# A two-stage attention and FFN kernel: the first tile's attention brought forward by one slot

## What is computed

```python
local_out  = softmax(q1 @ k1.T * scale) @ v1                          # full attention, one head of 128
sparse_out = softmax(top_k(q2 @ k2.T * scale, 102)) @ v2              # only the 102 largest scores of a row
mem_out    = [xp, softmax(xp @ bank.T) @ bank] @ mem_out_w + b        # 64 memory rows
pred_out   = gelu((h @ pred1_w + b)) @ pred2_w + b
s = concat(local_out, sparse_out, mem_out, pred_out) @ warboss_w + warboss_b
g = silu(relu(xn @ w1 + b1) @ w2 + b2)                                # FFN, width 2048
out = x + s * g
```

## Time and profile before

| what | value |
|---|---|
| median of 3 runs | 2587.35 us |
| profiled execution | 2589.47 us |
| its span (first to last instruction) | 2587.7 us |
| mean granted TensorE clock | 0.993 of full speed |
| chain that ended last | PE 94%, DVE 4%, DMA 1%, POOL 1% of the span |
| PE busy | 2535.0 us, 98% |
| DVE busy | 2317.5 us, 90% |
| ACT, POOL busy | 1363.0 us (53%), 1118.1 us (43%) |
| DMA | 558.60 MB, mean 216 GB/s |

### The profile page before, as it was taken

How to read it: one execution, slowest core, us unless ns; L and a number is a source line. 1 busy time by engine, 2 the same in 40 slices (tenths; PEclk the granted TensorE clock), 3 DMA queues, 4 the chain that set the end, 5 groups by cost and what they waited for, 6 DMA issues and landing times.

```text
span 2587.7 us, 37027 instructions
## 1 busy us (share of the span) xinstructions
PE 2535.0 (98%) x12900; PEld 2149.0 (83%) x12900; DVE 2317.5 (90%) x5194; ACT 1363.0 (53%) x2311; POOL 1118.1 (43%) x862
## 2 busy tenths in 40 slices
PE   6999999889999999999999999999999999999998
PEld 5888888778888888888888888888888888888886
DVE  7666666589999999999999999999999999999996
ACT  5777777634444444444444444444445454444443
POOL 4445554423444444444444444444444444444444
PEclk9999999989999999999999999999999999999999
DMA  6887788774566456645664566456645654565454
GB/s 217 302 306 296 294 311 305 294 267 155 196 213 217 163 196 214 214 166 196 216 215 164 196 215 214 165 197 215 214 164 196 213 210 163 196 230 200 165 201 166
DMA packets 166776, 558.60 MB, mean 216 GB/s; under 512 B 18048, under 2 KB 31040, under 8 KB 158144
## 3 DMA queue, kind: packets, MB, share of 16 engines
q1 hardware_dynamic: 166592, 556.24, 60.9%
HBM read 421.96 MB, written 134.22 MB: 215 GB/s over the span
## 4 chain that ended last, share of the span: by engine, by line
PE 94%; DVE 4%; DMA 1%; POOL 1%; ACT 0%; issue 0%; POOLq 0%; SPq 0%; ACTq 0%
PE acc L59 9%; PE acc L61 9%; PE acc L60 9%; PE hid L61 9%; PE hid L59 9%; PE hid L60 9%; PE ps L59 5%; PE ps L61 5%; PE ps L60 5%; PE o L59 5%; PE o L61 5%; PE o L60 5%; PE scores L1299 4%; PE scores L59 2%; PE scores L61 2%; PE scores L60 2%
## 5 line engine op out<-in xcount | busy, mean ns | idle before, releaser
L1052 POOL TENSOR_TENSOR h_lo<-h,h_hi 128x512 fp32r<-128x512 f32 x256 | 333.7, 1304 | 866.6 <-ACT h_hi L950 865.4
L1192 DVE MAX8 top_l<-larger 128x8 f32<-128x512 f32 x832 | 576.4, 693 | 13.2
L1212 DVE MATCH_REPLACE8 larger<-top_l,larger 128x512 f32<-128x512 f32 x768 | 521.6, 679 | 0.0
L949 ACT ACTIVATE h<-hid,small 128x512 f32<-128x512 f32 x256 | 176.5, 690 | 483.3 <-PE hid L61 483.3
L59 PE MATMUL acc<-w2s,h_hi 128*128 128x512 f32 x1024 | 412.1, 402 | 0.0
L59 PE MATMUL hid<-xnT,w 128*128 128x512 f32 x1024 | 400.3, 391 | 4.4 <-DMA w<-ffn_scratch 4.4
L61 PE MATMUL hid<-xnT,w 128*128 128x512 f32 x1024 | 400.5, 391 | 0.0
L61 PE MATMUL acc<-w2s,h_lo 128*128 128x512 f32 x1024 | 400.3, 391 | 0.0
L60 PE MATMUL acc<-w2s,h_hi 128*128 128x512 f32 x1024 | 400.2, 391 | 0.0
L60 PE MATMUL hid<-xnT,w 128*128 128x512 f32 x1024 | 400.0, 391 | 0.0
L1052 POOL TENSOR_TENSOR pT_s<-pT,pT_s 128x512 fp32r<-128x512 f32 x256 | 326.7, 1299 | 52.5 <-ACT pT_s L962 52.5
(11 more groups left out here) (175 smaller groups left out, 5593.5 us busy)
## 6 DMA issues: line engine op xcount, KB each, us to landing
w2s<-ffn_scratch SPq DMA_DIRECT2D x259, 512.0 KB, 3.9
w<-ffn_scratch SPq DMA_DIRECT2D x258, 512.0 KB, 4.2
tl<-tile_scratch SPq DMA_DIRECT2D x66, 512.0 KB, 3.9
xnT_scratch<-xnT SPq DMA_DIRECT2D x16, 2048.0 KB, 13.6
kv_scratch<-kv_out SPq DMA_DIRECT2D x32, 1024.0 KB, 5.6
tile_scratch<-tiles_out SPq DMA_DIRECT2D x16, 2048.0 KB, 8.3
xnT<-xnT_scratch SPq DMA_DIRECT2D x64, 512.0 KB, 7.0
xin<-in_L_attn_x SPq DMA_DIRECT2D x17, 1024.0 KB, 9.1
```

The costliest lines, as they stand in the source:

```text
L949: nc.scalar.activation(h32[:, c % 2, :], hid[:, :], ACT.Relu, bias=bias)
L1052: return nc.gpsimd.tensor_tensor(out_, value, hi_.bitcast(F32), ALU.subtract).then_inc(ready, 1)
L1192: l_step = count(nc.vector.max(top_l[:, own], larger[:, :]))
L1212: l_step = count(nc.vector.match_replace(larger[:, :], top_l[:, own], larger[:, :], LOWEST))
```

## The change

The attention of a tile runs one slot ahead of its FFN.

- The first tile's sparse scores are computed on PE after job `qs` of half 14, its local scores after job `pi` of half 15. DVE does its search in pieces between the jobs of these two halves (`first_search`, a generator, one round for each `next`): 1 round after gelu's low part of half 14, 3 after its `xnT` low parts, then 1, 1, 1, 2 and 4 rounds at five places of half 15. ACT copies the scores, and does both exponents and the scaling of the local ones.
- For this the `scores` banks, the search's tensors and the first inputs live through both stages (`Shared`). Stage 1 has 6 PSUM banks for its jobs instead of 8. `xin` and `xn` of stage 1 lie in the tensor `early`, which in stage 2 holds scores and probabilities. `xnT32` is gone; the transposed rows are written straight to where their low part goes (`xnT_raw`).
- The last half has no `tr` jobs; SP loads half 0's transposed rows back from scratch instead (`first_slot`), with `tl1` and `w1_0`. `tl0`, `ks` and `kl` are loaded in halves 13 and 14. The layer norms of halves 16 and 17, and their input loads, are gone. The last value part is made by POOL as the others are.
- Stage 2 runs slots 1 to 63 with the FFN chunks of F = m - 1, and a slot 64 that has only FFN chunks (4 f1, 5 f2) beside the last tile's transposes, products and mixes. `sums_of_half` moves with the FFN from slots with T modulo 4 = 0 to slots with T modulo 4 = 1. Gates and residuals are five slots behind instead of four. `mixed` has three buffers instead of two. Residuals of the last two tiles are done by DVE with their own input loads.

```diff
-BANKS = 8
+BANKS = 6
...
+    ORDER = [(n, name) for n in range(HALVES) for name in JOBS if n < LAST or name[:2] != "tr"]
+    PLACE = {job: KT + i for i, job in enumerate(ORDER)}
...
# stage 1, SP
-                        if n == LAST:
-                            load_first()
+                        if n == LAST:
+                            first_slot()
...
+                        if n == LAST - 2:
+                            first_tile()
+                        if n == LAST - 1:
+                            first_local()
...
# stage 1, ACT, after a job was read
+                            if (n, name) == (LAST - 1, "qs"):
+                                act.wait_ge(shared.ss_done, 1)
+                                nc.scalar.activation(shared.sc(), scores[:, :], ACT.Copy, scale=SCALE)\
+                                    .then_inc(shared.sc_ready, 1)
+                            if (n, name) == (LAST, "ms"):
+                                act.wait_ge(shared.nml_ready, 1)
+                                nc.scalar.activation(shared.prob(0), scores[:, :], ACT.Exp, bias=nml[:, :], scale=SCALE,
+                                                     accum_out=sums[:, 0:1]).then_inc(shared.el_ready, 1)
+                                act.wait_ge(shared.nms_ready, 1)
+                                nc.scalar.activation(shared.prob(1), shared.sc(), ACT.Exp, bias=nms[:, 0:1])\
+                                    .then_inc(shared.es_ready, 1)
+                            if (n, name) == (LAST, "qs"):
+                                act.wait_ge(shared.invl_ready, 1)
+                                nc.scalar.activation(shared.prob(0), shared.prob(0), ACT.Copy, scale=inv[:, 0:1])\
+                                    .then_inc(shared.pl_ready, 1)
...
# stage 1, DVE
+                        if n == LAST:
+                            dve.wait_ge(shared.sl_done, 1)
+                            nc.vector.tensor_reduce(mxl[:, :], scores[:, :], AX_X, ALU.max).then_inc(shared.nml_step, 1)
...
+                            next(rounds)
...
                         nc.vector.tensor_reduce(nmx[:, :], mscore[:, :, :], AX_X, ALU.max,
                                                 negate=True).then_inc(max_ready, 1)
+                        if n == LAST:
+                            next(rounds)
...
+                        if n == LAST:
+                            dve.wait_ge(shared.el_ready, 1)
+                            nc.vector.reciprocal(inv[:, 0:1], sums[:, 0:1]).then_inc(shared.invl_ready, 1)
+                            next(rounds)
                         dve.wait_ge(bank_read, done(n, "p1b"))
...
+                        if n == LAST:
+                            next(rounds)
+                            next(rounds)
                         dve.wait_ge(bank_read, done(n, "wt"))
...
# stage 1, PE, after a job
+                            if (n, name) == (LAST - 1, "qs"):
...
+                                first_scores(T_QS, shared.ks, shared.ss_done)
+                            if (n, name) == (LAST, "pi"):
...
+                                first_scores(T_QL, shared.kl, shared.sl_done)
...
# stage 2, SP, before the slots
                 load_w1(1, 1)
-                sp.wait_ge(tiles_st, 16 * 2 * B)
+                sp.wait_ge(tiles_st, 16 * HALVES)
                 load_w2(0, 0)
-                load_kv(U_KL, 0)
                 load_w2(1, 1)
-                load_tl(1, 1, 1)
-                sp.wait_ge(kv_st, 16 * 4 * B)
+                load_tl(2, 2, 2)
+                sp.wait_ge(kv_st, 32 * HALVES)
+                load_w2(2, 2)
+                load_kv(U_VL, 0)
...
# stage 2, DVE, search
-                        if r == R_SUMS and T % HTILES == 0 and not known_first(m, 1):
-                            sums_of_half(2 * b + T // HTILES - 1)
-                        if r == R_GATE and not known_first(m, HTILES):
-                            gates(m - HTILES, T % HTILES)
+                        if r == R_SUMS and T % HTILES == 1 and not known_first(m, 5):
+                            sums_of_half((m - 5) // HTILES)
+                        if r == R_GATE and not known_first(m, 5):
+                            gates(m - 5, (m - 5) % HTILES)
...
# stage 2, DVE, after slot 63
+                apply_threshold(SLOTS - 1, TILES - 1)
+                gates(SLOTS - 1 - HTILES, HTILES - 1)
+                mix(SLOTS - 2)
+                mix(SLOTS - 1)
+                sums_of_half(HALVES - 1)
                 for t in range(HTILES):
-                    gates((B - 1) * TILES + HTILES + t, t)
-                mix(B * TILES - 2, HTILES - 2)
-                mix(B * TILES - 1, HTILES - 1)
+                    gates(SLOTS - HTILES + t, t)
+                for m in range(SLOTS - 2, SLOTS):
+                    t = m % HTILES
+                    dve.wait_ge(gate_ready, m + 1)
+                    nc.vector.tensor_tensor(gate[:, t, :], gate[:, t, :], mixed_of(m), ALU.mult).then_inc(last_prod, 1)
...
+                    nc.vector.tensor_tensor(gate[:, t, :], gate[:, t, :], residual_of(m), ALU.add).then_inc(fin_last, 1)
...
# stage 2, PE, slot 64
+                f1(C, c, h)
                 pe.wait_ge(ps_ready, m - 1)
                 transposes(1)
-                f2(B * BC - 1, BC - 1, 2 * B - 1)
+                f2(C - 1, c - 1, h)
+                f1(C + 1, c + 1, h)
 
                 pe.wait_ge(pT_h, 4 * g + 2)
                 pe.wait_ge(ps_ready, m)
                 transposes(2)
+                f2(C, c, h)
+                f1(C + 2, c + 2, h)
                 pe.wait_ge(mix_ready, m - 2)
                 head_out(g, U_VS)
+                f2(C + 1, c + 1, h)
+                f1(C + 3, c + 3, h)
                 pe.wait_ge(at_l, g + 1)
                 mix(m - 2, (m - 2) % TL_RING)
+                f2(C + 2, c + 2, h)
                 pe.wait_ge(mix_ready, m - 1)
                 mix(m - 1, (m - 1) % TL_RING)
+                f2(C + 3, c + 3, h)
```

More of the change, by code:

```diff
@@ L538, in steps @@
+                rounds = first_search()
                 def steps(b):
@@ L607, in bank_projection, with first_scores @@
                     pe.wait_ge(sm_split, 2)
-                    product(nc, ps[:, BANKS - 1, 0:P], bkT_s[:, 0, :, :], bkT_s[:, 1, :, :], sm_hi[:, 1, :],
+                    product(nc, scores[:, 0:P], bkT_s[:, 0, :, :], bkT_s[:, 1, :, :], sm_hi[:, 1, :],
                             sm_lo[:, 1, :], True, True).then_inc(bm_ps, 1)
                 bank_projection()
+                def first_scores(slot, keys, ready):
+                    tl0 = shared.tl0
+                    for j in range(2):
+                        last = product(nc, scores[:, j * 512:(j + 1) * 512], tl0[:, HI, slot, :], tl0[:, LOW, slot, :],
+                                       keys[:, j, HI, :], keys[:, j, LOW, :], True, True)
+                    last.then_inc(ready, 1)
                 def steps(b):
@@ L928, in _ @@
+                for m in range(1, SLOTS + 1):
+                    slot(m)
+                for m in (SLOTS - 2, SLOTS - 1):
+                    load_x(m)
+                for m in range(SLOTS - HTILES, SLOTS):
+                    store(m)
                 for t in range(HTILES):
@@ L1037, in _, with slot @@
-                for b in range(B):
-                    slots(b)
-                last = B * TILES - 1
+                def slot(m):
+                    T, F = m % TILES, m - 1
+                    C = c = HC * F
+                    sparse_scores(m, T % 2)
+                    chunk(C, c)
+                    sparse_probabilities(m - 1, 1 + (T - 1) % 2)
+                    transposed(m - 1, 0)
+                    chunk(C + 1, c + 1)
+                    if T % 2 == 0:
+                        transposed(m - 1, 1)
+                        sparse_exponents(m, T)
+                        if not known_first(m, 5):
+                            gates(m - 5, (m - 5) % HTILES)
+                        chunk(C + 2, c + 2)
+                        local_exponents(m)
+                        head_out(m - 1, 1)
+                        local_probabilities(m)
+                    else:
+                        sparse_exponents(m, T)
+                        if not known_first(m, 5):
+                            gates(m - 5, (m - 5) % HTILES)
+                        local_exponents(m)
+                        local_probabilities(m)
+                        chunk(C + 2, c + 2)
+                        transposed(m - 1, 1)
+                    chunk(C + 3, c + 3)
+                    if T % 2 == 1:
+                        head_out(m - 1, 0)
@@ L1040, in _ @@
+                for m in range(1, SLOTS):
+                    slot(m)
+                last = SLOTS - 1
+                C = c = HC * last
+                chunk(C, c)
                 sparse_probabilities(last, 1 + last % 2)
                 transposed(last, 0)
+                chunk(C + 1, c + 1)
                 transposed(last, 1)
-                for t in range(2):
```

(31 more changed lines are left out.)

680 lines of the change are left out of this document (356 added, 324 removed).

## The result

| | before | after |
|---|---|---|
| median of the runs, us | 2587.35 | 2598.54 |
| lowest and highest | 2586.85 to 2587.92 | 2597.91 to 2600.36 |
| profiled execution: its time, span | 2589.47, 2587.7 | 2600.15, 2598.3 |
| slots 5, 9, ... 61, us each | 32.00 to 32.08 | 33.43 to 33.45 |
| the other slots from 2 on | 31.88 to 31.93 | 31.88 to 31.93 |

The change makes the kernel slower: the ratio is 1.0045, with a 95% interval of 1.0033 to 1.0057. The forecast was 2593.4 us, with a range of 2580 to 2601. So the direction holds, and the size is +11.2 us where +6.0 was forecast.

What follows compares the result with a forecast made beforehand. PE was taken to set the time in mid stage 2, with DVE 2.4% behind. Terms +19.1 (sums), 0 (banks), -31.6 (boundary) and +18.5 (tail) gave +6.0 on 2587.35, so 2593.4 us, range 2580 to 2601.

Steps and rivals of the forecast that it cites:

- Part 1, the sums: Middle of stage 2: sums delay the maximum, so PE waits in 15 odd slots, 1.27 us each, +19.1 us.
- The sum of "about 21 us" for the waits: Slots 5, 9, ... 61: a sign to look for, 15 waits of the transposes for the scaling, about 21 us together.
- Part 2, the banks: Stage 1: six banks instead of eight cost 0, since the closest pair of jobs has 1.1 us to spare.
- Part 3, the stage boundary: Last two halves to slot 2: stage 2 begins at 512.2, slot 2 at 546.8 instead of 578.43, -31.6 us.
- the forecast wait: Slot 1: PE waits for the weights of chunk 2, which land at 530 behind 9 MB in the queue.
- Part 4, the tail: Slot 64 takes 34.7 us without a wait, then a chain of 12.7 us to the end: +18.5 us.
- The rival of the port lock: Tail: up to three DVE operations each wait out one of POOL, 3.5 us longer, 2597 us; chance 0.08.
- the absorbed sums: Slots 5 to 61: scaling comes at least 1.4 us earlier, the +19.1 is 0, 2574.3 us; chance 0.13.
- the better boundary: Stage boundary: weights land early or the last half stalls less, -3.3 us, 2590 us; chance 0.12.
- the banks: Rival in stage 1: ACT reads later than 1.1 us allow, 0.5 us in 16 halves, +8, 2601 us; chance 0.05.

Runs made afterwards that it cites:

- experiments 4 and 5: Changed kernel, in slots 5, 9, ... 61: sums behind the local maximum, 2592.0 us; then maximum, sums and reciprocal before the fourth round's MAX8, 2591.7 us.
- experiment 2: Kernel before, with four extra MAX8 on DVE in the even slots 2, 6, ... 62: 2605.3 us.
- experiment 3: Kernel before, with six PSUM banks instead of eight for the jobs of stage 1: 2588.1 us, ratio 1.0001.
- Experiment 7: Changed kernel, with DVE beginning the first tile's search in half 14 behind the low parts of wt and xnT: 2596.3 us.
- experiments 8 and 11: 8: changed kernel, first tile's exponents behind mo of half 15, scaling at the half's end, reciprocal behind the search, 2596.2 us; experiment 11 has its own line.
- experiment 9: Changed kernel, with two tanh buffers in turn for the last four tiles: 2598.5 us.
- experiment 10: Changed kernel with two tanh buffers, and POOL's last two residuals done by DVE: 2597.3 us.
- experiment 6: Experiment 5's kernel (see experiments 4 and 5), with DVE copying the mix two rounds earlier in slots 5, 9, ... 61: 2576.1 us, ratio 0.9955 to the kernel before.
- experiment 11: Changed kernel with the edits of experiment 6, Experiment 7, 8 and experiment 10 joined, and wt's low part ahead of the rounds: 2570.9 us, ratio 0.9935.

## Why the prediction was right, and where its sizes were off

**Part 1, the sums.** Right in place, number and mechanism: 15 waits at the transposes for the scaling. The slots became 33.44 - 31.92 = 1.52 us longer, less the 0.08 to 0.16 us that such slots paid before: 1.40 instead of 1.27, and 21.0 us instead of 19.1. What failed is a small step: I took what the transposes' start is delayed by for the whole lengthening of the slot. That delay was right. The transposes start 21.40 us into slot 61 and 19.97 into slot 63, which has no sums: 1.43 us later, 1.39 forecast. The maximum comes 2.38 us later in its slot (2.33 forecast), and the slack was 0.99. But behind the wait the slot gets another 0.08 us longer, most of it at the transposes themselves (the next matmul starts 0.85 us behind their start instead of 0.79). The sum of "about 21 us" for the waits was a little high, 19.2 / 15 = 1.28 us each, because a recorded idle time starts at the shown end of a matmul: matmuls stand 0.23 us apart and each is shown 0.39 us long, so 0.16 us is missed. In experiments 4 and 5 slots are 1.03 us longer with 0.71 and 0.77 us recorded. The reading of DVE's slack was right for one slot, but as a reading of the whole it was too generous: 2.4% was called spare, and the waits of the kernel before come to 0.9%; experiment 2 shows that the rest can't be had.

**Part 2, the banks.** 0, as forecast (experiment 3).

**Part 3, the stage boundary.** -29.0 us measured in this pair of traces (-29.6 between the averages of four traces with the old boundary and six with the new) instead of -31.6. Two steps failed, in opposite directions, and largely cancelled.

- Stage 2 was to begin at 512.2. It began at 518.18, 6.0 us later (SP's first load is issued at 518.00). Of these, 3.8 us come before `mo` of half 15, which starts at 504.63 and not at 500.8, and 2.2 us behind it. First, half 14: I gave it no cost. But there PE waits 1.75 us for a low part, and half 15 begins at 477.02, 2.9 us later than forecast; 1.5 us of that is the low clock of this one trace. Experiment 7 shows that the wait was made by where the search begins. Second, I counted 0.77 us for DVE's low part of `wt`, and it lasted 2.04 us; the two pair operations in half 14 lasted 1.77 and 1.78 us instead of 0.7. Third, I put low clock only behind the wait for `w`. From `mo` to stage 2 I had 11.4 us, and it took 13.55: behind the 3.63 us without work, PE's granted clock was 0.50 from 504 to 510 us.
- PE was to wait for `w` until 530. The weights of chunk 2 were issued at 525.25 and landed 7.5 us later, at 532.75, later than forecast, and PE came at 533.80, 1.05 us after them. So the wait never came, and slot 1 took 31.23 us instead of 34.6. The transfers bound nothing even when PE came 4 to 5 us earlier (experiments 8 and 11), since the issue of those weights waits for PE's own first chunk: it comes 7 us into slot 1 in all three.

That the second error took back 3.4 of the 6.0 us is luck. With the forecast wait behind the late start, the time would have been some 2602 us, outside the range (an estimate: 2598.5 + 3.4).

The page DMA: Bandwidth & Descriptors of the Trainium skill, section Two DMAs through the same engine are not ordered, allows the weights to overtake the values. Here the values, issued at 522.42, landed 9.1 us later at 531.5, 1.25 us ahead of the weights, so no overtaking is seen at the place where it would have counted, and no run forced one. But the trace of before has a landing that shows it, and I had missed it: at the program's start a small load issued at 8.89 us landed 4.9 us later, and one issued at 9.55 landed 4.1 us later, so it came 0.2 us sooner than the older one.

**Part 4, the tail.** +18.6 us measured, +18.5 forecast. Slot 64 took 34.6 us without a wait (34.7 forecast), the rest 12.9 (12.7). The gates stand 1.4 to 1.9 us apart, where the earlier trace rows gave 1.56. The four gates took 5.9 us (5.6 forecast) and the four operations behind them 3.7 (3.2), against 0.4 us set aside for POOL and a last sum that was 0.2 us shorter. The gate at 2587.61 took 1.13 us, and one operation behind them was slowed by 1.06 us:

```profile
2589.50 0.92 DVE L1310 SCALAR_TENSOR_TENSOR gate<-th,gate 128x512 f32<-128x512 f32 x1 [0.76 <-ACT th L1157]
2591.18 0.92 DVE L1310 SCALAR_TENSOR_TENSOR gate<-th,gate 128x512 f32<-128x512 f32 x1 [0.76 <-ACT th L1157]
2592.02 1.75 DVE L1415 TENSOR_TENSOR gate<-gate,mixed 128x512 f32<-128x512 f32 x1
```

The rival of the port lock (+3.5) had the right mechanism and the wrong count. The gates waited for ACT's tanh anyway, and so one operation was slowed by a whole POOL operation instead of three. Where that wait was taken away, four were slowed (experiment 9), and where POOL's residuals were taken away too, none (experiment 10).

**The sum.** 21.0 - 29.0 + 18.6 = 10.6 us against 6.0. The middle is off by 1.9 us, the boundary by 2.6; between the medians of the runs the change is 11.2. The rivals: the absorbed sums (13 in 100) didn't come by themselves, but experiment 6 shows that they can be had, at 2576.1 instead of the 2574.3 worked out for them; the better boundary and the banks are ruled out.

Left open: slot 2's start varies by over 2 us between kernels whose stage 1 is the same. The traces show where: in half 14 the clock fell in one of them (1.5 us), and from `mo` of half 15 to stage 2 they take 12.6 to 14.1 us, with a granted clock of 0.50 to 0.72 from 503 to 509 us. Why the clock falls in one and not in another isn't shown, nor how much of experiment 11's boundary could still be had; no run was made for either.

## What to carry to other kernels

Work that is added ahead of a value with a due time costs what exceeds the slack of that one value, however idle its engine is on average. Put it behind the value, then look at the next due of the same engine: here three dues stood in a row, at the transposes, at the product with the sums and at the mix. They cost 1.5, 1.0 and 1.0 us a slot until the last was met, and the first two fixes alone gave less than a third of the gain. Judge an engine's room by how long and in which slots it waits, not by one minus its busy time. And look at a clock in several traces before you put it down to the edit: here the low clock behind a wait was there in one of seven.

## What the runs showed of the hardware

- Operations of DVE that read two tensors of SBUF take up to one POOL operation longer beside POOL: 0.69 became 1.5 to 1.78 us. In experiment 11 the low part of `wt`, 0.77 us alone, took 2.75 us beside a POOL operation of 1024 columns, which took 3.36 itself, and a cast of 1024 columns went from 0.69 to 1.73. MAX8, MATCH_REPLACE8 and the maximum over PSUM didn't change: from 600 to 2540 us of the changed kernel, the 780 MAX8 of L1357 have a median of 0.69 us whether they lie beside a POOL operation or not, and none takes more than 0.70. The Trainium skill, SBUF — State Buffer, section Who interferes with whom, puts the line just there (two SBUF inputs, or a copy or cast in a two-port mode, against a lock on the shared pair); the trace agrees.
- A wait of PE doesn't always lower its clock. In half 14 PE stood for 1.75 us at `mo` in the changed kernel, and for 1.74 to 1.76 us in six others with the same half. In the changed kernel the granted clock from 468 to 473 us was 0.66, partly at the lower level of 1.2 GHz, although PE was busy for 4.84 of the 5 us; in the six it was 1.00, the level of 2.4 GHz. Behind the 3.63 us without work at `mo` of half 15, it was 0.50 from 504 to 510 us.
